# Units of one pair of edge steps, one-step message multiplies, later masks and a shifted step table in a graph-and-mixer kernel

## The chip, the cores and the metric

The kernel runs on one core of a Trainium2 chip. The metric is device time in microseconds (us); smaller is better. Everything is in fp32.

## The reference

The input `x` has 3125 rows (nodes) of 256 values. There are 53,125 edges, each with a source row, a destination row (the list is sorted by destination) and one of 400 relation types. `xn` is `x`, layer-normalised.

```python
def _mgcn_conv(x, edge_index, edge_type, rel, W_in, W_out, W_loop, b, n):
    m = x[src] * rel[edge_type]
    m = jnp.concatenate([m[:half] @ W_in, m[half:] @ W_out], 0)
    agg = jax.ops.segment_sum(m * norm[dst][:, None], dst, num_segments=n)
    return jnp.tanh(agg + x @ W_loop + b)
h = emb + res * _mgcn_conv(emb, ..., rel1, ...)
h = h + res * _mgcn_conv(h, ..., rel2, ...)
return h @ mu_w + mu_b
```

To this graph part, run on `xn`, are added `x` itself and the result of a mixer on `xn`: four layers, each of a linear attention (queries by softmax over a head's 32 columns, keys by softmax over all 3125 rows, one 32x32 context a head) and a feed-forward of 1024 hidden columns with gelu. On the sum `x`, layer-normalised once more, a last block of one shared three-layer network and four small expert networks (the two best by a softmax gate) gives what is added at the end.

## The kernel before

**Tiles.** The nodes stand in 25 tiles of 125 rows, in five groups of five. The mixer goes layer by layer (0 to 3) and in a layer group by group: `iteration(lay, gi)`, called (lay, gi) below. Ahead of each layer stands a joint, `joint(la)`, in which the context over all rows is closed and turned into weights (joint 1 stands between layers 0 and 1), and ahead of joint 0 the fronts (queries, keys and values of layer 0, one for each group). The last stage (the last block, with the second dense part of the graph) runs over slots `s = 1..26`, one tile each.

**Edges.** Each of the two graph layers (g=0 and g=1) has 416 steps of 128 edges. For a step POOL gathers 128 node rows into a ring of 16 slots by an indirect DMA (L1049: `xg<-xn_rows` for g=0, `xg<-h_rows` for g=1). For g=0 it also gathers 128 rows of relations, of both layers side by side (L1001, `rg<-relation_rows`). SP stores the second half of these to DRAM (L875, L892) and loads them back for g=1 (L917). A unit was `UNIT = 4` steps, in two pairs: one step of each pair belongs to the first 64 rows of a window of 125 nodes, the other to the last 61. For a unit DVE writes a one-hot table of its 4x64 rows (L1128, `hot`; for the first units also `hot_extra`, L1132), waits for the unit's gathers and multiplies the rows by the relations, in one instruction of 128x1024 (L1143). PE then sums the rows into windows by the one-hot table (L2735, `ps_seg`): for a pair two matmuls side by side, 64 and 61 columns wide, where its other matmuls are 125 or 128 wide. When they are done the unit's four ring slots are free for POOL (`s_seg`). Once a window is complete DVE adds it to `acc`, for each tile that it meets under a mask from the table `in_tile` (L1117).

**Order.** Every engine's order is written out. The numbers of steps beside each front, joint, group and the last stage stand in tables (`STEPS_FRONT`, `STEPS_JOINT`, `STEPS_GROUP`, `STEPS_LAST`), divided by `UNIT`; `marks`, `joint_marks`, `front_marks` and `last_units` spread a group's units over places in its work. DVE makes its units one unit ahead of PE (`units_ahead`, L738). g=0 ends in (2,3), where `AMONG` units stand among the 25 tiles of its dense part (`dense_behind`); g=1 begins in (2,4) (`dense_before`) and ends in the last stage.

**Masks.** `in_tile` needs 36 small subtractions, one for each window (L2100, 125x2), and two operations on the whole table (L2103, L2105). They stand in DVE's prologue, ahead of three `k_max` and two `norm` of the fronts (L1205, L1346). The first add that reads the table is some units later.

**Last stage.** In each slot DVE makes `gated_rows` (L2151), a share of units, and so on. For the next group of tiles its last normalisation is made in three steps: `last_stats` (L1902), at slot s when tile s+3 opens a group, and one slot later `last_root` (L1908 and the small ops of `inv_sqrt`, L548 to L567) with `last_rows` (L1918, which writes `acc`). PE transposes `acc` as the group's first work (L607).

Of the kernel before, what the change touches and what calls it, by code (L numbers as in the profile page):

```python
# [9 lines left out]
ALU = mybir.AluOpType  # L10
# [15 lines left out]
RING = 16  # L26
SLOTS = 3
CUT = 112
UNIT = 4
HOT_UNITS = 2  # L30
ROUND = 2
WIN = 6
BLOCK = 4
HEADSTART = 16
STORE_AT = (2, 5)
STRIPS = ((0, 64), (64, T))
# [3 lines left out]


STEPS_FRONT = (0, 8, 8, 8, 8)
STEPS_JOINT = (16, 16, 16, 32)
STEPS_GROUP = ((16, 24, 24, 24, 24), (16, 24, 24, 24, 24), (16, 24, 24, 48, 48), (24, 52, 52, 52, 52))
STEPS_LAST = 104
AMONG, AMONG_AT, AMONG_EVERY = 6, 3, 3
DENSE_LAYER, DENSE_GROUP = 2, 4
LAG = 18

# [1 line left out]
def build(nc, io, out):  # L51
# [133 lines left out]
    with ExitStack() as ctx:  # L185
# [540 lines left out]

        def among(t):

            return min(max((t - AMONG_AT) // AMONG_EVERY + 1, 0), AMONG)

        def dense_loads(h):

# [327 lines left out]
        def _(dve):  # L1060
# [36 lines left out]
            class Edges:  # L1097
# [23 lines left out]
                def unit(self):  # L1121
# [17 lines left out]
                    else:  # L1139
                        dve.wait_ge(s_edge[k % RU], (k // RU + 1 + 2 * (UNITS // RU)) * (16 * UNIT))  # L1140
                        dve.wait_ge(s_r2ld[k % RU], (k // RU + 1) * 16)
                        r = rg2[:, s:s + UNIT, :]
                    dve.tensor_tensor(m, m, r, ALU.mult).then_inc(s_msg, 1)  # L1143
                    while self.adds < adds_before(k):
                        self.add()
                    for _ in range(2):
# [292 lines left out]
            def front_tiles(f, before, after, m, upto, one):  # L1439

                if before:
                    before.k_max(GT - 1)
                f.norm(2)
                upto(m[0])
                f.norm(3)
                f.norm(4)
                if before:
                    before.q_max()
                    before.k_top()
                    before.q_shift()  # L1450
                upto(m[1])
                if before:
                    before.k_shift()
                f.k_max(1)
                upto(m[2])
                if before:
                    before.q_sum()
                    before.q_scale()
                f.k_max(2)
                upto(m[3])  # L1460
                if not after:
                    f.q_max(0)
                    f.q_shift(0)
                f.k_max(3)
                if after:
                    after.norm(0)
                    after.norm(1)
                upto(m[4])
                if before:
                    before.add_context()  # L1470
                if not after:
                    f.q_sum(0)
                    f.k_max(GT - 1)
                    f.q_scale(0)
# [620 lines left out]
            dve.wait_ge(s_ppe, 7)  # L2095
            p(dve.tensor_copy(starts, ps_in[0:T, 0:WINS]))
            p.wait()
            for w in range(WINS):
                a, found = in_tile_at[w], blocks_of(w)
                p(dve.tensor_scalar(in_tile[:, a:a + len(found)], row_of[:, found.start:found.stop], starts[:, w:w + 1], None,  # L2100
                                    ALU.subtract))
            p.wait()
            p(dve.tensor_scalar(below, in_tile[:, :], 0.0, None, ALU.is_ge))  # L2103
            p.wait()
            p(dve.scalar_tensor_tensor(in_tile[:, :], in_tile[:, :], strip_width, below, ALU.is_lt, ALU.mult))  # L2105
            p.wait()
            dve.sem_inc(s_tab, 1)
            fronts[0].k_max(2)
            fronts[0].k_max(3)
            fronts[1].norm(0)  # L2110
            fronts[1].norm(1)
            dve.wait_ge(s_zero, 2)

            at, edges = 0, Edges(0)
            for ga in range(1, NG):
# [55 lines left out]
            for s in range(1, NT + 2):  # L2171
# [21 lines left out]
                if gi and j == 0:  # L2193
                    softmax(gi)
                    top_two(gi)
                    gates(gi)
                if last_part(s + 3)[1] == 0:
                    rooted = last_stats(last_part(s + 3)[0])
                if last_part(s + 2)[1] == 0:
                    last_root(rooted)  # L2200
                    last_rows(last_part(s + 2)[0])


        @block.scalar
# [1318 lines left out]
```

## Time and profile before

| what | value |
|---|---|
| runs of the kernel | 1978.4 us median of 3 (1976.6 to 1980.3) |
| the profiled execution, its own time | 1990.7 us |
| its span in the trace | 1988.9 us |
| busy: PE, DVE, POOL, ACT | 1771.3, 1183.3, 1335.6, 627.8 us |
| mean granted TensorE clock | 0.961 of full |

The page gives for each engine how long it was busy, then the chain of work that ended last, then the costliest groups of instructions with what ended the idle time before them. A stretch view gives the same for a piece of the span, a timeline each instruction with its start, its duration and, in brackets, the idle time of its engine before it and what ended that. An instruction of PE stands in the timeline from its issue to its modelled end, so that consecutive rows overlap; for PE the distance from start to start is read.

### The profile page before, as it was taken

To read this page: it belongs to the slowest core of one execution; us is meant where nothing else is said; L and a number is where in the kernel's file an instruction comes from. 1 tells how busy PE (TensorE), PEld (TensorE's weight loads), DVE (VectorE), ACT (ScalarE), POOL (GpSimd) and SP (SyncE) were. 2 spreads that over 40 slices of the span, in tenths; PEclk is the share of its full clock that TensorE was granted. 3 is DMA by queue.
4 is the path that set the end of the run, shared out by engine and by line. 5 is a ranking of instruction groups with operands and counts; after the bars stand their busy time and mean duration, and the time that the engine had idled before them with its cause. 6 is when DMAs were issued, how large, how long until landed. Compare 5 with 4: busy or idle time off the path is not lost.

```text
span 1988.9 us, 27738 instructions
## 1 busy us (share of the span) xinstructions
PE 1771.3 (89%) x9423; PEld 1303.9 (66%) x9423; DVE 1183.3 (59%) x2959; ACT 627.8 (32%) x1552; POOL 1335.6 (67%) x1297
## 2 busy tenths in 40 slices
PE   2788899998899999989999879878989898988988
PEld 1455777776587777658777546646656665766778
DVE  6766455564755556474655554585455465577755
ACT  4442233443323344332333233232221222222333
POOL 6776777777777777777777716755677566677200
PEclk9898999999899999999999999998999998989989
DMA  9667666667766666776667755758656556555201
GB/s 256 185 200 238 200 186 204 187 197 217 235 196 194 205 195 192 243 217 196 193 197 218 233 146 169 226 182 221 185 185 202 162 176 189 160 175 183 82 14 27
DMA packets 195918, 371.40 MB, mean 187 GB/s; under 512 B 39343, under 2 KB 127445, under 8 KB 195780
## 3 DMA queue, kind: packets, MB, share of 16 engines
q0 software_dynamic: 74304, 220.71, 38.3%
q1 hardware_dynamic: 93124, 126.68, 20.0%
q10 hardware_dynamic: 28352, 22.24, 4.1%
q8 instruction: 78, 1.28, 0.3%
q14 instruction: 60, 0.49, 0.1%
HBM read 305.39 MB, written 64.95 MB: 186 GB/s over the span
## 4 chain that ended last, share of the span: by engine, by line
PE 43%; POOL 26%; issue 10%; DVE 10%; DMA 4%; SPq 2%; ACT 1%; ACTq 1%; DVEq 0%; POOLq 0%
POOL xg L1049 16%; POOL rg L1001 10%; PE ps_down L2876 8%; PE ps_hid L2864 7%; PE ps_seg L2735 5%; PE ps_x L607 2%; PE ps_hid L3358 2%; DMA xg<-h_rows,idx_tab 2%; PE ps_kv L2773 2%; DVE xg L1143 2%; PE ps_x L2828 2%; SPq L788 2%; PE ps_down L2906 1%; PE ps_kv L2906 1%; DMA h_rows<-qT_all 1%
## 5 line engine op out<-in xcount | busy, mean ns | idle before, releaser
L1049 POOL DMA_INDIRECT xg<-h_rows,idx_tab x416 | 444.7, 1069 | 208.6 <-issue 119.6
L1049 POOL DMA_INDIRECT xg<-xn_rows,idx_tab x416 | 437.7, 1052 | 133.4 <-issue 125.5
L1001 POOL DMA_INDIRECT rg<-relation_rows,idx_tab x416 | 429.5, 1033 | 136.4 <-issue 126.1
L2864 PE MATMUL ps_hid<-hT,wff 128*128 128x250 f32 (+1 forms) x1920 | 370.9, 346 | 9.1 <-ACT gT L2298 9.1
L2876 PE MATMUL ps_down<-wff,gT 128*125 128x256 f32 x1600 | 373.0, 387 | 0.0
L2864 PEld LDWEIGHTS ps_hid<-hT,wff 128*128 128x128 f32 x1920 | 313.4, 192 | 60.6 <-issue 28.4
L2876 PEld LDWEIGHTS ps_down<-wff,gT 128*125 128x125 f32 x1600 | 300.1, 192 | 48.8 <-issue 5.1
L1143 DVE TENSOR_TENSOR xg<-xg,rg 128x1024 f32<-128x1024 f32 x208 | 253.7, 1220 | 128.8 <-DMA rg<-relation_rows,idx_tab 67.3
L2298 ACT ACTIVATE gT<-ps_hid,b1p 128x250 f32<-128x250 f32 (+1 forms) x480 | 176.4, 433 | 294.2 <-PE ps_hid L2864 294.1
L2735 PE MATMUL ps_seg<-xg,hot 128*64 128x257 f32 (+1 forms) x1664 | 232.9, 404 | 34.8 <-DVE xg L1143 31.8
L2735 PEld LDWEIGHTS ps_seg<-xg,hot 128*64 128x64 f32 (+1 forms) x1664 | 102.6, 139 | 131.2 <-issue 57.3
L1128 DVE TENSOR_TENSOR hot<-iota_t,key_tab 128x256 f32<-128x256 f32 x208 | 87.0, 418 | 64.8 <-PE ps_seg L2735 63.2
L2773 PE MATMUL ps_kv<-wqkv,hTa 128*125 128x512 f32 x240 | 115.7, 604 | 1.8 <-ACT hTa L2238 1.8
L2209 ACT ACTIVATE kx<-ps_kv 125x256 f32<-125x256 f32 x72 | 27.7, 384 | 233.3 <-PE ps_kv L2773 221.8
L1117 DVE SCALAR_TENSOR_TENSOR acc<-ps_seg,in_tile,acc 125x257 f32<-125x257 f32 x194 | 93.2, 480 | 3.0
L1323 DVE TENSOR_TENSOR xres<-xres,ps_down 125x256 f32<-125x256 f32 x100 | 39.9, 416 | 90.7 <-PE ps_down L2876 90.1
L1265 DVE TENSOR_TENSOR xres<-xres,ps_x 125x256 f32<-125x256 f32 x80 | 30.7, 416 | 95.2 <-PE ps_x L2828 95.1
L2284 ACT ACTIVATE hT<-ps_x,ln2p 128x250 f32<-128x250 f32 (+1 forms) x120 | 56.1, 525 | 98.6 <-PE ps_x L607 93.8
L2828 PE MATMUL ps_x<-cwo,qT_all 128*125 128x256 f32 x320 | 82.1, 396 | 0.0
L1205 DVE TENSOR_TENSOR kmax<-kmax,kx 125x256 f32<-125x256 f32 x54 | 22.8, 422 | 83.6 <-ACT kx L2209 83.0
L2773 PEld LDWEIGHTS ps_kv<-wqkv,hTa 128*125 128x125 f32 x240 | 43.6, 189 | 41.6 <-issue 37.1
L2828 PEld LDWEIGHTS ps_x<-cwo,qT_all 128*125 128x125 f32 x320 | 57.7, 191 | 20.0 <-issue 12.8
(382 smaller groups left out, 2435.7 us busy)
## 6 DMA issues: line engine op xcount, KB each, us to landing
second_relation_rows<-rg SPq DMA_DIRECT2D x104, 512.0 KB, 4.1
rg<-second_relation_rows SPq DMA_DIRECT2D x104, 512.0 KB, 3.9
wff<-L_mix_W ACTq DMA_DIRECT2D x8, 1024.0 KB, 7.4
rg<-relation_rows,idx_tab POOLq DMA_INDIRECT x416
xg<-xn_rows,idx_tab POOLq DMA_INDIRECT x416
xg<-h_rows,idx_tab POOLq DMA_INDIRECT x416
h_rows<-qT_all SPq DMA_DIRECT2D x25, 64.0 KB
qrow<-h_rows ACTq DMA_DIRECT2D x25, 64.0 KB
```

Of the source, the lines that this page charges most:

```text
L1001: pool.indirect_dma_start(rg[:, k, :], None, rel_d, indices(step, 1)).then_inc(s_edge[k // UNIT], 16)
L1049: pool.indirect_dma_start(xg[:, k, 0:D], None, rows, indices(step, 0)).then_inc(s_edge[k // UNIT], 16)
L1117: dve.scalar_tensor_tensor(a, ps_seg[bank_of(w)][0:T, 0:AW], in_tile[:, m:m + 1], a, ALU.mult, ALU.add).then_inc(s_acc, 1)
L1128: dve.tensor_tensor(hot[:, hs:hs + UNIT, :], iota_t[:, :].unsqueeze(1).broadcast_to([EP, UNIT, WIDTH[0]]), key_tab[:, at:at + UNIT].unsque ...
L1143: dve.tensor_tensor(m, m, r, ALU.mult).then_inc(s_msg, 1)
L2284: ins = act.activation(hT[:, j:z, c, :], turned[:, :, c * T:(c + 1) * T], ACT.Identity, bias=ln2p[:, 1, c:c + 1], scale=ln2p[:, 0, c:c + 1])
L2298: ins = act.activation(out, hidden, ACT.Gelu, bias=b1p[:, ff:ff + 1])
L2735: ins = pe.matmul(ps_seg[bank_of(w)][a:z, 0:AW], hot[:, u % HOT_UNITS * UNIT + part, 0:z - a], xg[:, u % RU * UNIT + part, :], start=now = ...
L2773: ins = pe.matmul(ps_kv[0:T, :], hTa[:, j % 2, c, :], wqkv[:, c, 0:2 * D], start=c == 0, stop=c == KC - 1)
L2828: ins = pe.matmul(ps_b[j % 2][0:T, :], q[:, c * T:(c + 1) * T], cwo[:, c, :], start=c == 0, stop=c == KC - 1)
L2864: ins = pe.matmul(hidden, w1[:, c, ff * P:(ff + 1) * P], hT[:, a:z, c, :], start=c == 0, stop=c == KC - 1)
L2876: ins = pe.matmul(ps_down[j % 2][0:T, :], gT[:, j % 2, f, :], w2[:, f, :], start=f == 0, stop=f == FC - 1)
```

## The change

- `UNIT` 4 to 2: a unit is one pair of steps. The ring has 8 units in place of 4 (`RU`), `HOT_UNITS` 2 to 4 and `BLOCK` 4 to 2 keep the buffers at their size, and SP stores and loads 208 blocks of 256 KB in place of 104 of 512 KB. DVE's lead of one unit is now 2 steps.
- The message multiply is one instruction of 128x256 for each step, in place of 128x1024 for four.
- Layer 2's steps beside its last group, and layer 3's: joint 3 32 to 20 steps, (2,4) 48 to 52, (3,0) 24 to 36, (3,1) 52 to 40, (3,2) to (3,4) 52 to 56 each, the last stage 104 to 100. `AMONG` 6 to 12 keeps its 24 steps, at twice the units a tile.
- The masks move from the prologue into front 1: 12 after its `norm(4)`, 12 after `k_max(1)`, the rest and the two whole-table operations after `k_max(2)`.
- In the last stage `last_stats`, `last_root` and `last_rows` stand one slot earlier.

```diff
--- before.py
+++ after.py
@@ -26,11 +26,11 @@
 RING = 16
 SLOTS = 3
 CUT = 112
-UNIT = 4
-HOT_UNITS = 2
+UNIT = 2
+HOT_UNITS = 4
 ROUND = 2
 WIN = 6
-BLOCK = 4
+BLOCK = 2
 HEADSTART = 16
 STORE_AT = (2, 5)
 STRIPS = ((0, 64), (64, T))
@@ -40,10 +40,10 @@
 
 
 STEPS_FRONT = (0, 8, 8, 8, 8)
-STEPS_JOINT = (16, 16, 16, 32)
-STEPS_GROUP = ((16, 24, 24, 24, 24), (16, 24, 24, 24, 24), (16, 24, 24, 48, 48), (24, 52, 52, 52, 52))
-STEPS_LAST = 104
-AMONG, AMONG_AT, AMONG_EVERY = 6, 3, 3
+STEPS_JOINT = (16, 16, 16, 20)
+STEPS_GROUP = ((16, 24, 24, 24, 24), (16, 24, 24, 24, 24), (16, 24, 24, 48, 52), (36, 40, 56, 56, 56))
+STEPS_LAST = 100
+AMONG, AMONG_AT, AMONG_EVERY = 12, 3, 3
 DENSE_LAYER, DENSE_GROUP = 2, 4
 LAG = 18
 
@@ -726,7 +726,7 @@
 
         def among(t):
 
-            return min(max((t - AMONG_AT) // AMONG_EVERY + 1, 0), AMONG)
+            return min(max((t - AMONG_AT) * 2 // AMONG_EVERY + 1, 0), AMONG)
 
         def dense_loads(h):
 
@@ -1140,7 +1140,9 @@
                         dve.wait_ge(s_edge[k % RU], (k // RU + 1 + 2 * (UNITS // RU)) * (16 * UNIT))
                         dve.wait_ge(s_r2ld[k % RU], (k // RU + 1) * 16)
                         r = rg2[:, s:s + UNIT, :]
-                    dve.tensor_tensor(m, m, r, ALU.mult).then_inc(s_msg, 1)
+                    for i in range(UNIT):
+                        ins = dve.tensor_tensor(m[:, i, :], m[:, i, :], r[:, i, :], ALU.mult)
+                    ins.then_inc(s_msg, 1)
                     while self.adds < adds_before(k):
                         self.add()
                     for _ in range(2):
@@ -1444,6 +1446,8 @@
                 upto(m[0])
                 f.norm(3)
                 f.norm(4)
+                if f.ga == 1:
+                    make_masks(12)
                 if before:
                     before.q_max()
                     before.k_top()
@@ -1452,11 +1456,15 @@
                 if before:
                     before.k_shift()
                 f.k_max(1)
+                if f.ga == 1:
+                    make_masks(12)
                 upto(m[2])
                 if before:
                     before.q_sum()
                     before.q_scale()
                 f.k_max(2)
+                if f.ga == 1:
+                    make_masks(WINS)
                 upto(m[3])
                 if not after:
                     f.q_max(0)
@@ -2095,21 +2103,29 @@
             dve.wait_ge(s_ppe, 7)
             p(dve.tensor_copy(starts, ps_in[0:T, 0:WINS]))
             p.wait()
-            for w in range(WINS):
-                a, found = in_tile_at[w], blocks_of(w)
-                p(dve.tensor_scalar(in_tile[:, a:a + len(found)], row_of[:, found.start:found.stop], starts[:, w:w + 1], None,
-                                    ALU.subtract))
-            p.wait()
-            p(dve.tensor_scalar(below, in_tile[:, :], 0.0, None, ALU.is_ge))
-            p.wait()
-            p(dve.scalar_tensor_tensor(in_tile[:, :], in_tile[:, :], strip_width, below, ALU.is_lt, ALU.mult))
-            p.wait()
             dve.sem_inc(s_tab, 1)
             fronts[0].k_max(2)
             fronts[0].k_max(3)
             fronts[1].norm(0)
             fronts[1].norm(1)
             dve.wait_ge(s_zero, 2)
+
+            masks = [w for w in range(WINS)]
+
+            def make_masks(n):
+
+                for _ in range(min(n, len(masks))):
+                    w = masks.pop(0)
+                    a, found = in_tile_at[w], blocks_of(w)
+                    ins = dve.tensor_scalar(below[:, a:a + len(found)], row_of[:, found.start:found.stop], starts[:, w:w + 1], None,
+                                            ALU.subtract)
+                    if not masks:
+                        p(ins)
+                        p.wait()
+                        p(dve.tensor_scalar(in_tile[:, :], below, 0.0, None, ALU.is_ge))
+                        p.wait()
+                        p(dve.scalar_tensor_tensor(in_tile[:, :], below, strip_width, in_tile[:, :], ALU.is_lt, ALU.mult))
+                        p.wait()
 
             at, edges = 0, Edges(0)
             for ga in range(1, NG):
@@ -2194,11 +2210,11 @@
                     softmax(gi)
                     top_two(gi)
                     gates(gi)
+                if last_part(s + 4)[1] == 0:
+                    rooted = last_stats(last_part(s + 4)[0])
                 if last_part(s + 3)[1] == 0:
-                    rooted = last_stats(last_part(s + 3)[0])
-                if last_part(s + 2)[1] == 0:
                     last_root(rooted)
-                    last_rows(last_part(s + 2)[0])
+                    last_rows(last_part(s + 3)[0])
 
 
         @block.scalar
```

PE in group (1,1) of layer 1, before; L2864 and L2876 are the two halves of the feed-forward:

```order
L2864 MATMUL ps_hid<-hT,wff 128x250 x8
L2735 MATMUL ps_seg<-xg,hot 64x257
L2735 MATMUL ps_seg<-xg,hot 61x257
L2735 MATMUL ps_seg<-xg,hot 64x257
L2735 MATMUL ps_seg<-xg,hot 61x257
L2864 MATMUL ps_hid<-hT,wff 128x250 x8
L2735 MATMUL ps_seg<-xg,hot 64x257
L2735 MATMUL ps_seg<-xg,hot 61x257
L2735 MATMUL ps_seg<-xg,hot 64x257
L2735 MATMUL ps_seg<-xg,hot 61x257
L2876 MATMUL ps_down<-wff,gT 125x256 x8
```

The same place now (the lines are 16 further down):

```order
L2880 MATMUL ps_hid<-hT,wff 128x250 x4
L2751 MATMUL ps_seg<-xg,hot 64x257
L2751 MATMUL ps_seg<-xg,hot 61x257
L2880 MATMUL ps_hid<-hT,wff 128x250 x4
L2751 MATMUL ps_seg<-xg,hot 64x257
L2751 MATMUL ps_seg<-xg,hot 61x257
L2880 MATMUL ps_hid<-hT,wff 128x250 x8
L2751 MATMUL ps_seg<-xg,hot 64x257
L2751 MATMUL ps_seg<-xg,hot 61x257
L2892 MATMUL ps_down<-wff,gT 125x256 x8
L607 MATMUL ps_x<-ident,kx 128x125 x2
```

The two units of two pairs each are four units of one pair, each alone between other matmuls: where PE went over to the narrow shape and back twice, it now does so four times.

DVE in layer 1, before; L1198, L1205, L1265 and L1323 are work of the mixer:

```order
L1198 TENSOR_SCALAR kx<-xres,mv,rstd 125x256
L1128 TENSOR_TENSOR hot<-iota_t,key_tab 128x256
L1143 TENSOR_TENSOR xg<-xg,rg 128x4x256
L1198 TENSOR_SCALAR kx<-xres,mv,rstd 125x256
L1205 TENSOR_TENSOR kmax<-kx 125x256
L1265 TENSOR_TENSOR xres<-xres,ps_x 125x256 x2
L1323 TENSOR_TENSOR xres<-xres,ps_down 125x256
L1198 TENSOR_SCALAR kx<-xres,mv,rstd 125x256
L1205 TENSOR_TENSOR kmax<-kmax,kx 125x256
L1128 TENSOR_TENSOR hot<-iota_t,key_tab 128x256
L1143 TENSOR_TENSOR xg<-xg,rg 128x4x256
L1117 SCALAR_TENSOR_TENSOR acc<-ps_seg,in_tile,acc 125x257 x3
```

The same place now:

```order
L1200 TENSOR_SCALAR kx<-xres,mv,rstd 125x256
L1128 TENSOR_TENSOR hot<-iota_t,key_tab 128x128
L1144 TENSOR_TENSOR xg<-xg,rg 128x256 x2
L1128 TENSOR_TENSOR hot<-iota_t,key_tab 128x128
L1144 TENSOR_TENSOR xg<-xg,rg 128x256 x2
L1200 TENSOR_SCALAR kx<-xres,mv,rstd 125x256
L1207 TENSOR_TENSOR kmax<-kx 125x256
L1267 TENSOR_TENSOR xres<-xres,ps_x 125x256 x2
L1325 TENSOR_TENSOR xres<-xres,ps_down 125x256
L1200 TENSOR_SCALAR kx<-xres,mv,rstd 125x256
L1207 TENSOR_TENSOR kmax<-kmax,kx 125x256
L1128 TENSOR_TENSOR hot<-iota_t,key_tab 128x128
```

The table of a unit is 128x128 in place of 128x256, and its multiply two instructions of 128x256 in place of one of 128x1024; other work of DVE stands between the two halves of what was a unit, or the halves follow each other.

DVE at the second group of the last stage, before:

```order
L1128 TENSOR_TENSOR hot<-iota_t,key_tab 128x256
L1143 TENSOR_TENSOR xg<-xg,rg 128x4x256
L1871 SCALAR_TENSOR_TENSOR qrow<-kx,singles,qrow 125x256
L1879 TENSOR_TENSOR xres<-xres,ps_kv 125x256
L1847 TENSOR_SCALAR kmax<-acc,norm 125x256
L2167 TENSOR_TENSOR xres<-xres,ps_down 125x256
L2161 SCALAR_TENSOR_TENSOR xres<-kx,xres 125x256 x4
L1908 BN_AGGR mv<-stat 125x2 x5
L548 TENSOR_SCALAR var<-mv 125x5
```

The same step now (L1908 is now L1916, L2151 is now L2167, L1863 and L1871 are 8 further down):

```order
L1128 TENSOR_TENSOR hot<-iota_t,key_tab 128x128
L1144 TENSOR_TENSOR xg<-xg,rg 128x256 x2
L1117 SCALAR_TENSOR_TENSOR acc<-ps_seg,in_tile,acc 125x257
L1128 TENSOR_TENSOR hot<-iota_t,key_tab 128x128
L1144 TENSOR_TENSOR xg<-xg,rg 128x256 x2
L1871 TENSOR_TENSOR kx<-ps_kv,gb 125x256
L2183 TENSOR_TENSOR xres<-xres,ps_down 125x256
L2177 SCALAR_TENSOR_TENSOR xres<-kx,xres 125x256 x4
L1916 BN_AGGR mv<-stat 125x2 x5
L548 TENSOR_SCALAR var<-mv 125x5
```

The aggregation stood behind the `qrow` rows of a dense tile in the slot of the third `gated_rows`; it now stands in the slot of the second, behind the `kx<-ps_kv` row that precedes them.

## Rows read from the trace of the kernel before

**Rows 1.** The page: busy time by engine, and the chain by engine.

```profile
PE 1771.3 (89%) x9423; PEld 1303.9 (66%) x9423; DVE 1183.3 (59%) x2959; ACT 627.8 (32%) x1552; POOL 1335.6 (67%) x1297
...
PE 43%; POOL 26%; issue 10%; DVE 10%; DMA 4%; SPq 2%; ACT 1%; ACTq 1%; DVEq 0%; POOLq 0%
```

**Rows 2.** Stretches: start:end, length, busy us (instructions) by engine, PEclk, DMA share, GB/s.

```profile
320.00:385.00 65.00, 63.46 (x321) 47.64 (x320) 38.83 (x96) 25.05 (x60) 50.42 (x48) 1.00 0.66 195
655.80:719.00 63.20, 62.87 (x319) 47.47 (x319) 38.87 (x95) 24.97 (x59) 48.89 (x47) 1.00 0.67 197
...
1405.00:1500.00 95.00, 79.20 (x417) 57.54 (x416) 47.46 (x94) 16.37 (x41) 72.58 (x68) 0.93 0.65 201
1720.00:1989.00 269.00, 237.24 (x1659) 197.71 (x1657) 180.15 (x484) 79.50 (x262) 98.05 (x88) 0.93 0.33 100
1758.40:1765.10 6.70, 3.89 (x15) 2.05 (x16) 5.98 (x19) 1.14 (x3) 5.15 (x5) 0.50 0.38 103
```

**Rows 3.** Waits of PE in 1405 to 1500 and in 1720 to 1989: total, times, longest.

```profile
PE ps_seg L2735 <- DVE xg L1143: 11.2, 6, 2.5
...
PE ps_down L607 <- DVE acc L1918: 12.2, 4, 4.8
```

**Rows 4.** Groups by line: busy us, mean ns, idle before by releaser.

```profile
L1049 POOL DMA_INDIRECT xg<-h_rows,idx_tab x416 | 444.7, 1069 | 208.6 <-issue 119.6 <-PE ps_seg L2735 84.4 <-DMA h_rows<-qT_all 4.6
L1049 POOL DMA_INDIRECT xg<-xn_rows,idx_tab x416 | 437.7, 1052 | 133.4 <-issue 125.5 <-PE ps_seg L2735 6.4 <-DMA xn_rows<-xres 1.5
L1001 POOL DMA_INDIRECT rg<-relation_rows,idx_tab x416 | 429.5, 1033 | 136.4 <-issue 126.1 <-DVE idx_tab L1083 10.0 <-DMA xn_rows<-xres 0.3
...
L1143 DVE TENSOR_TENSOR xg<-xg,rg 128x1024 f32<-128x1024 f32 x208 | 253.7, 1220 | 128.8 <-DMA rg<-relation_rows,idx_tab 67.3 <-DMA xg<-h_rows,idx_tab 57.9 <-DMA xg<-xn_rows,idx_tab 3.0
```

**Rows 5.** Timeline 690.9 to 696: start, us, engine, line, op, [idle before <-releaser].

```profile
691.26 0.94 POOL L1049 DMA_INDIRECT xg<-xn_rows,idx_tab  x1 [0.30 <-issue]
...
692.45 1.22 DVE L1143 TENSOR_TENSOR xg<-xg,rg 128x1024 f32<-128x1024 f32 x1
692.51 1.98 POOL L1001 DMA_INDIRECT rg<-relation_rows,idx_tab  x1 [0.30 <-issue]
```

**Rows 6.** Timeline 713 to 716, DVE and POOL.

```profile
713.72 0.42 DVE L1128 TENSOR_TENSOR hot<-iota_t,key_tab 128x256 f32<-128x256 f32 x1
713.84 1.12 POOL L1001 DMA_INDIRECT rg<-relation_rows,idx_tab  x1 [0.30 <-issue]
714.06 1.22 DVE L1143 TENSOR_TENSOR xg<-xg,rg 128x1024 f32<-128x1024 f32 x1
```

**Rows 7.** Timeline 604 to 612 and 620 to 646, PE.

```profile
604.53 3.62 PE L2876 MATMUL ps_down<-wff,gT 128*125 128x256 f32 x16
...
608.08 1.09 PE L2735 MATMUL ps_seg<-xg,hot 128*64 128x257 f32 x8
...
609.09 1.99 PE L2828 MATMUL ps_x<-cwo,qT_all 128*125 128x256 f32 x8
...
641.49 3.62 PE L2876 MATMUL ps_down<-wff,gT 128*125 128x256 f32 x16
...
644.94 0.38 PE L607 MATMUL ps_x<-ident,xh 125*128 125x125 f32 x2
```

**Rows 8.** Timeline 45 to 60, the prologue on DVE and PE.

```profile
47.81 4.81 DVE L2100 TENSOR_SCALAR in_tile<-qT_all 125x2 f32<-125x2 f32 x36
...
54.73 0.40 PE L607 MATMUL ps_x<-ident,wff 125*128 125x125 f32 x2 [3.84 <-DVE wff L1346]
```

**Rows 9.** Timeline 480 to 492, the second joint.

```profile
484.13 1.23 DVE L1143 TENSOR_TENSOR xg<-xg,rg 128x1024 f32<-128x1024 f32 x1 [9.83 <-DMA rg<-relation_rows,idx_tab]
...
486.84 0.79 PE L2785 MATMUL ps_kv<-ident,ktop 128*125 128x128 f32 x2 [5.57 <-DVE ktop L1212]
```

**Rows 10.** Timeline 1757 to 1762.5, the last stage.

```profile
1760.64 1.84 DVE L1918 TENSOR_SCALAR acc<-xres,mv,rstd 125x256 f32<-125x256 f32 x5
...
1761.11 0.68 PE L607 MATMUL ps_down<-ident,acc 125*128 125x125 f32 x2 [4.83 <-DVE acc L1918]
```

## The prediction

> **What bounds the kernel now.** I read the page first: PE is busy for 1771.3 us of the span of 1988.9, POOL for 1335.6, DVE for 1183.3, and the chain that ended last runs 43% over PE and 26% over POOL's gathers [rows 1]. PE is idle for 1988.9 - 1771.3 = 217.6 us; this is all that better timing can give back. Then I read the stretches [rows 2]. An iteration of layer 0 takes 65.0 us with PE busy for 63.46, one of layer 1 63.2 with 62.87: layer 1 is bound by PE, layer 0 nearly so. In layer 3's first part PE is busy for 79.20 of 95 us at a granted clock of 0.93, in the last stage for 237.24 of 269. So the reader should see two kinds of stretch: full ones, in which extra PE work is paid and nothing is gained by faster gathers, and loose ones, in which a wait can go.
>
> **Why gathers are slow.** The three groups of gathers mean 1069, 1052 and 1033 ns [rows 4], where an undisturbed one takes 0.94 with 0.30 of gap [rows 5]. Together they are (129 + 112 + 93) ns x 416 = 139 us over 0.94 each. The timeline shows one reason: the gather at 692.51, begun 0.06 us after a message multiply of 1.22, takes 1.98, and so ends 0.82 after the multiply's end, as if it had waited for that end [rows 5]. The gather at 713.84, begun under `hot`, takes only 1.12, though the multiply follows `hot` 0.34 us later: it got in between two instructions that stand back to back [rows 6].
>
> **The change, part by part.** Sums are against the profiled execution, 1990.7 us (1988.9 of span); it stands 12.3 above the median of 1978.4, and I carry differences over.
>
> *One-step multiplies on POOL.* A gather that ends 0.82 after the multiply loses nothing if it begins in the last 0.94 - 0.82 = 0.12 us of it. One that begins in the 1.10 before loses half of that on the mean; with one gather in 1.25 us this is 1.10 x 1.10 / 2 / 1.25 = 0.48 us a multiply, 101 us for 208, an estimate. Four pieces of 0.42 (as `hot`, a 256-wide one [rows 6]) cost 4 x 0.30 x 0.30 / 2 / 1.25 = 0.14, 30 us. Saved: up to 71 us of POOL; as the rows hold only 139 for all causes I take 60, half in each graph layer. The lower bound is 0, if gathers don't get in between. In full stretches this is worth nothing; in loose ones it is counted below.
>
> *One-step multiplies and smaller tables on DVE.* From start to start `hot` occupies 0.34 [rows 6], the multiply 1.22 - 0.08 = 1.14, with the overlap of 0.08 that `hot` has. Four pieces take 4 x 0.34 = 1.36, +0.22; two tables of 128x128 in place of one of 128x256 cost between 0 and another 0.34, and I take 0.06, since a narrower one should be shorter. So 208 x 0.28 = +58 us busy, between 46 and 117, on an engine busy for 60%. It hides beside PE; where DVE feeds PE directly, joint 3 and the last stage with 120 steps (30 of the old units), it is 30 x 0.28 = 8 at most, and as DVE waits there as well I allow +3. The Trainium skill, page "VectorE: DVE Perf Modes", section "The TRN2 errata — SBUF-src ops pay a fixed extra latency per instruction", speaks against this part: many small tiles each pay a fixed price, so that by its formula (151 + N columns at 0.96 GHz, an estimate) four pieces would take 1.70 us, +98 us busy in all. All on the path in those 30 units, that would be +14 in place of +3, and with the factor of two thirds below the forecast 1962. The row's 0.34 from start to start shows part of that price hidden behind the instruction before.
>
> *Units of one pair on PE.* Sixteen full-width matmuls followed by others of full width take 644.94 - 641.49 = 3.45; followed by a unit 608.08 - 604.53 = 3.55; so going over costs 0.10. The unit takes 609.09 - 608.08 = 1.01, where four pairs at the 3.45 / 16 = 0.216 of a full matmul would be 0.86: 0.15 more [rows 7]. Coming back I take as going over, 0.10: 0.35 us a run of units. Counted in PE's order, runs that stand alone rise from 194 to 303: +109, or +38 us of PE, 83 of them (29 us) in g=0. The bounds are 0.10 (11 us) and 0.45 (49 us). The Trainium skill, page "TensorEngine Tiling (Array Packing)", section "Key Properties", says that a change of tiling mode drains the array; the rows agree, with these 0.35 us.
>
> *Masks.* PE's wait of 3.84 in the prologue is for `wff` of L1346, which stands behind the 36 masks (4.81) [rows 8]. -4, all of that wait; the 4.81 go into front 1 beside POOL's gathers and cost up to 5 there if PE waits for that front's `k_max`.
>
> *g=0.* Prologue -4. Joints 0 and 1, 2 and group (0,1) are loose: in joint 1 DVE stands for 9.83 behind a multiply for its gathers and PE for 5.57 for the `ktop` behind it [rows 9]. POOL gains some 30 us over g=0, 10 of them by then: I take -6 there, and -7 for the other places of this kind (waits for relation rows are 67.3 us in all, the 9.83 among them [rows 4]). In layer 0 the 1.54 us that PE idles in an iteration pay for five runs more (1.75): 0. Layer 1 is full: 5 x 1.7 = +8. The rest of the runs stand beside other waits: +3. Sum -6.
>
> *g=1.* POOL waits for free slots for 84.4 us in g=1 [rows 4]; moving 12 steps from (3,1) to (3,0), and 12 out of joint 3, puts gathers where the ring stands empty, and units of two steps free slots twice as often. In 1405 to 1500, (3,1), PE idles for 15.8 us, 11.2 of them for the multiply that waits for gathers [rows 2, 3]: 12 steps fewer at 1.25 are 15 us of POOL: -15. (2,4) and joint 3: -6, of the same 84.4. The other groups -2. Last stage: PE waits 12.2 us in 4 times for L1918 [rows 3], once for 4.83 us right behind it [rows 10], and after it the clock stands at 0.50 for 6.7 us with 3.89 busy [rows 2]. One slot of 269 / 25 = 10.8 us earlier covers this; -12, and half of the busy time of two or three such spells, 2 to 6, as -5: -17. Runs +5, DVE +3. Sum -32.
>
> Together -38. Each wait that goes shows what was late behind it (PE idles for 217.6, and other terms take only a sixth of this), and DVE's lead of two steps in place of four costs, below, nothing, and above, ten more waits like the 11.2 / 6 = 1.9 us of PE for the multiply [rows 3], 20. As no row excludes either, I keep two thirds of the gain, -24: **1954.4 us**.
>
> **The rivals.**
> - *PE pays for the runs and gets nothing back in g=0.* The +38 us fall where PE is the bound; joints wait for other things than POOL. For it: layer 1 is full, and 83 of 109 runs are in g=0 [rows 2]. Then g=0 is -4 + 29 = +25, g=1 with half its gains -13: +12, 1990. It decides once the recovered waits are under the 38 us of the runs. This is the slower side.
> - *Gathers don't get in between the pieces.* Four multiplies back to back hold them off like one of 1.22. The page "SBUF — State Buffer" of the Trainium skill, section "🔬 SBUF: two separate sides", has a lock held for a whole instruction, which speaks for a gap at its end, as does the gather at 713.84 [rows 6]. Without the 13 of the joints and a third of the 21 in layer 3, times two thirds: -24 + 13 = -11, 1967.
> - *DVE's lead is too short.* PE comes to a unit whose gathers and multiply are not quite done, twice as many units as before; a dozen more waits of 1.9 us [rows 3] eat the 24: 0, 1978. It decides from there on.
> - *All waits go at once*, with the half clock behind them: -38 and 12 more where the clock of 0.93 in the two loose stretches rises [rows 2] (0.07 x 316 us of busy PE is 22, of which 10 are counted): -50, 1928.
>
> **How the numbers follow.** My forecast (1942 to 1968) has 0.46; all waits at once 0.12; gathers held off 0.14; the short lead 0.10, which splits over no change (0.07) and slightly slower (0.03); PE's runs 0.18, of them 0.01 within no change. A measurement can tell 0.2%, 4 us. So faster 0.46 + 0.12 + 0.14 = 0.72, same 0.08, slower 0.20. The range reaches from the case of all waits to that of the runs, 1928 to 1990, a little out at the low end for the POOL saving's bound: 1925 to 1990. The likeliest case's own range is 1942 to 1968.
>
> **What would show it.** Right: gathers near 0.97 us on the mean, few of 1.5 or more; PE's wait for L1918 gone and the clock 1.0 there; 1405 to 1500 with PE over 90% busy; the iteration of layer 1 longer by 1 to 2 us; PE's busy time up by about 30; DVE's by 46 to 60. Wrong: PE waiting for L1143 (now 208 pairs) longer in all than before, or gathers as long as now, or a layer 0 that doesn't shrink anywhere while layer 1 grows by 8.

## The result, and the profile after

The changed kernel takes 1992.0 us (median of 9 runs, 1987.7 to 2001.0), the kernel before 1980.3 in the same comparison (9 runs, 1975.7 to 1990.0). The ratio is 1.0062, 95% interval 1.0037 to 1.0087: **slower by 0.6%, 12 us**, where 1954 was forecast.

The two traces don't show this at a glance: the profiled execution of before (1990.7) was one of its slowest, that of the change (1988.6) one of its fastest. Differences of stretches are good to some ten microseconds in all, and medians decide on the whole. First the page's busy times of the change, then its groups by line, the answer to [rows 1, 4]:

```profile
PE 1796.5 (90%) x9423; PEld 1284.9 (65%) x9423; DVE 1236.0 (62%) x3803; ACT 629.7 (32%) x1552; POOL 1293.8 (65%) x1297
```

```profile
L1001 POOL DMA_INDIRECT rg<-relation_rows,idx_tab x416 | 427.6, 1028 | 135.9 <-issue 126.1 <-DVE idx_tab L1083 9.4 <-DMA xn_rows<-xres 0.3
L1049 POOL DMA_INDIRECT xg<-xn_rows,idx_tab x416 | 424.0, 1019 | 131.0 <-issue 120.0 <-PE ps_seg L2751 5.5 <-DMA xn_rows<-xres 4.6
L1049 POOL DMA_INDIRECT xg<-h_rows,idx_tab x416 | 418.6, 1006 | 251.4 <-PE ps_seg L2751 135.0 <-issue 109.8 <-DMA h_rows<-qT_all 6.3
...
L1144 DVE TENSOR_TENSOR xg<-xg,rg 128x256 f32<-128x256 f32 x832 | 313.8, 417 | 26.5 <-DMA xg<-h_rows,idx_tab 13.5 <-DMA rg<-relation_rows,idx_tab 6.5 <-DMA xg<-xn_rows,idx_tab 5.4
...
L2751 PE MATMUL ps_seg<-xg,hot 128*64 128x257 f32 (+1 forms) x1664 | 263.6, 412 | 66.7 <-DVE xg L1144 63.4 <-DVE acc L1117 1.7 <-DVE acc L1114 1.3
```

PE is busy for 1796.5 us in place of 1771.3, and idle for 190 in place of 218. The gathers are shorter by 41.7 us together (418.6 + 424.0 + 427.6 against 1311.9). But PE's waits for a message multiply (L1144, before L1143) are now 63.4 us, where they were 31.8: the prediction had named longer waits there as a sign of being wrong.

To find where the time went I followed the same matmuls of PE through both traces. The change is ahead by 13 us at the end of group (0,1), by 25 behind joint 1, by 18 behind layer 1 and by 44 where the last stage's matmuls begin, at 1665.1 in place of 1709.2. Then it loses all of it. These are stretches of the change: an iteration of layer 0, one of layer 1, the part of layer 3 that stood at 1405 to 1500, and the last stage (start:end, length, busy us (instructions) of PE, PEld, DVE, ACT and POOL, then PEclk, DMA share, GB/s):

```profile
306.00:370.90 64.90, 64.57 (x321) 47.01 (x320) 40.47 (x121) 25.02 (x58) 50.28 (x49) 1.00 0.67 194
630.00:694.80 64.80, 64.47 (x320) 47.01 (x321) 40.37 (x120) 25.27 (x59) 49.82 (x49) 1.00 0.67 200
1383.60:1461.20 77.60, 75.71 (x419) 54.51 (x418) 49.19 (x154) 17.57 (x45) 55.76 (x54) 1.00 0.69 204
1665.10:1986.80 321.70, 261.90 (x1712) 211.47 (x1710) 189.59 (x587) 81.28 (x267) 89.58 (x92) 0.91 0.30 86
```

And of the kernel before, cut at the same matmuls, an iteration of layer 1, the part of layer 3 and the last stage:

```profile
651.10:714.30 63.20, 62.87 (x319) 47.47 (x319) 38.84 (x96) 24.97 (x59) 48.89 (x48) 1.00 0.66 197
1405.00:1502.10 97.10, 81.30 (x427) 59.31 (x426) 47.88 (x95) 16.37 (x41) 74.24 (x70) 0.93 0.65 199
1709.20:1988.90 279.70, 248.04 (x1716) 206.52 (x1714) 182.73 (x490) 82.38 (x267) 104.19 (x95) 0.93 0.33 100
```

Layer 1's iteration went from 63.2 to 64.8, layer 0's stayed (65.0 before [rows 2]), layer 3's piece went from 97.1 us with a clock of 0.93 to 77.6 at full clock. **The last stage went from 279.7 to 321.7: +42 us**, with PE idle for 60 us in place of 32. The waits in it, of the change (total, times, longest):

```profile
POOL xg L1049 <- PE ps_seg L2751: 80.9, 26, 6.8
DVE xh L2167 <- PE ps_x L3455: 69.2, 21, 5.8
...
PE ps_seg L2751 <- DVE xg L1144: 47.3, 25, 5.9
```

Before, the wait of the last row was, in the last stage:

```profile
PE ps_seg L2735 <- DVE xg L1143: 5.1, 5, 2.0
```

A timeline of two places in it (start, us, engine, line, op, [idle before <-releaser]):

```profile
1699.03 0.65 PE L2751 MATMUL ps_seg<-xg,hot 128*64 128x257 f32 x4
...
1700.59 1.72 DVE L1910 BATCH_NORM_STATS2 stat<-xres 125x6 f32<-125x256 f32 x5
...
1702.42 0.76 DVE L1144 TENSOR_TENSOR xg<-xg,rg 128x256 f32<-128x256 f32 x2
...
1703.29 0.76 DVE L1144 TENSOR_TENSOR xg<-xg,rg 128x256 f32<-128x256 f32 x2
1703.32 0.65 PE L2751 MATMUL ps_seg<-xg,hot 128*64 128x257 f32 x4 [3.64 <-DVE xg L1144]
...
1716.18 0.65 PE L2751 MATMUL ps_seg<-xg,hot 128*64 128x257 f32 x4
...
1717.55 0.44 DVE L1916 BATCH_NORM_AGGREGATE mv<-stat 125x2 f32<-125x6 f32 x5
...
1720.14 1.70 DVE L1926 TENSOR_SCALAR acc<-xres,mv,rstd 125x256 f32<-125x256 f32 x5
...
1721.97 0.75 DVE L1144 TENSOR_TENSOR xg<-xg,rg 128x256 f32<-128x256 f32 x2
...
1722.77 1.12 PE L2751 MATMUL ps_seg<-xg,hot 128*64 128x257 f32 x4 [5.94 <-DVE xg L1144]
```

A slot of this stage has two places for units (`last_units`), one in each half. A half slot has some two units of two steps where it had one of four, and the lead of one unit covers only the first. PE's first matmuls of a pair run at once (1699.03, 1716.18). For the second PE stands until DVE has come to the next pair of units: behind five statistics (1700.59) it waits for 3.64, and behind the chain of the earlier normalisation (1717.55 to 1720.14 and 1.70 more) for 5.94, after which a unit takes nearly twice as long (1.12 for 0.65). The granted clock of the stretch behind it is 0.58, so that most of it ran at the lower level of 1.2 GHz:

```profile
1722.70:1729.40 6.70, 6.63 (x34) 5.80 (x36) 0.90 (x5) 1.69 (x6) 1.89 (x2) 0.58 0.41 117
```

DVE for its part stands for a matmul of PE further on in the slot (L2167, 69.2 us), and POOL for free ring slots (80.9).

### The profile page after: what moved, and what is told of

The parts are those of the page before. It is cut to its first block and busy times, and to the rows that moved or that the text cites. A ratio compares the mean times of both kernels' runs of the same rounds, so it can differ in the third digit from the quotient of the medians.

```text
span 1986.8 us, 29094 instructions
## 1 busy us (share of the span) xinstructions
PE 1796.5 (90%) x9423; PEld 1284.9 (65%) x9423; DVE 1236.0 (62%) x3803; ACT 629.7 (32%) x1552; POOL 1293.8 (65%) x1297
## 5 line engine op out<-in xcount | busy, mean ns | idle before, releaser
L1049 POOL DMA_INDIRECT xg<-h_rows,idx_tab x416 | 418.6, 1006 | 251.4 <-PE ps_seg L2751 135.0
L1001 POOL DMA_INDIRECT rg<-relation_rows,idx_tab x416 | 427.6, 1028 | 135.9 <-issue 126.1
L1049 POOL DMA_INDIRECT xg<-xn_rows,idx_tab x416 | 424.0, 1019 | 131.0 <-issue 120.0
L2880 PE MATMUL ps_hid<-hT,wff 128*128 128x250 f32 (+1 forms) x1920 | 381.3, 349 | 6.6 <-ACT gT L2314 6.3
L2892 PE MATMUL ps_down<-wff,gT 128*125 128x256 f32 x1600 | 363.2, 380 | 0.0
L1144 DVE TENSOR_TENSOR xg<-xg,rg 128x256 f32<-128x256 f32 x832 | 313.8, 417 | 26.5 <-DMA xg<-h_rows,idx_tab 13.5
L2751 PE MATMUL ps_seg<-xg,hot 128*64 128x257 f32 (+1 forms) x1664 | 263.6, 412 | 66.7 <-DVE xg L1144 63.4
L2892 PEld LDWEIGHTS ps_down<-wff,gT 128*125 128x125 f32 x1600 | 293.2, 188 | 45.4 <-issue 5.1
L2751 PEld LDWEIGHTS ps_seg<-xg,hot 128*64 128x64 f32 (+1 forms) x1664 | 90.2, 137 | 183.3 <-issue 82.3
L1128 DVE TENSOR_TENSOR hot<-iota_t,key_tab 128x128 f32<-128x128 f32 x416 | 117.7, 283 | 25.0 <-PE ps_seg L2751 23.4
L1117 DVE SCALAR_TENSOR_TENSOR acc<-ps_seg,in_tile,acc 125x257 f32<-125x257 f32 x194 | 93.2, 481 | 38.6 <-PE ps_seg L2751 30.9
```

The source lines that it names most:

```text
L1001: pool.indirect_dma_start(rg[:, k, :], None, rel_d, indices(step, 1)).then_inc(s_edge[k // UNIT], 16)
L1049: pool.indirect_dma_start(xg[:, k, 0:D], None, rows, indices(step, 0)).then_inc(s_edge[k // UNIT], 16)
L1117: dve.scalar_tensor_tensor(a, ps_seg[bank_of(w)][0:T, 0:AW], in_tile[:, m:m + 1], a, ALU.mult, ALU.add).then_inc(s_acc, 1)
L1128: dve.tensor_tensor(hot[:, hs:hs + UNIT, :], iota_t[:, :].unsqueeze(1).broadcast_to([EP, UNIT, WIDTH[0]]), key_tab[:, at:at + UNIT].unsque ...
L1144: ins = dve.tensor_tensor(m[:, i, :], m[:, i, :], r[:, i, :], ALU.mult)
L2751: ins = pe.matmul(ps_seg[bank_of(w)][a:z, 0:AW], hot[:, u % HOT_UNITS * UNIT + part, 0:z - a], xg[:, u % RU * UNIT + part, :], start=now = ...
```

## The experiments

All ratios are to the kernel before, 1975.8 to 1977.5 us in these comparisons. Runs 1, 4, 6 and 8 were measured together, so were 3, 7, 9 and the first of 11, and 2, 5, 10 and the second of 11; across these sets the ratios compare better than the medians.

**1. Two units of lead in the last stage.**

```diff
-            upto, _ = edges.stage(at_last, 1)
+            upto, _ = edges.stage(at_last, 2)
```

> DVE makes its units two units (four steps) ahead of PE in the last stage, as many steps as in the kernel before; all else as in the change. If the short lead is what costs the 42 us that the change loses in the last stage, PE's waits there for the multiply (47.3 us in 25 times) fall under 15 and the time falls by 30 to 45, to 1947 to 1962, below the kernel before. If the normalisation one slot earlier is the cause, or the runs of units on PE, the waits stay and the time stays within 6 us of 1992.

Measured: 1946.6 us, ratio 0.982 (0.979 to 0.986). PE's instructions and their order are those of the change; only DVE makes its units earlier. Its last stage, and PE's wait in it:

```profile
1670.30:1945.60 275.30, 248.58 (x1712) 203.29 (x1710) 188.65 (x587) 81.83 (x267) 91.93 (x92) 0.94 0.34 100
```

```profile
PE ps_seg L2751 <- DVE xg L1144: 14.3, 8, 4.1
```

275.3 us in place of 321.7, the wait 14.3 in place of 47.3. This one number turns the change from 0.6% slower into 1.8% faster than the kernel before: the lead is what made it slower.

**2. The adds alone.** The change with its lead of one unit, and DVE's window adds (L1117) allowed only four units behind its own unit, which is eight steps as in the kernel before:

```diff
-                        if self.adds < ADDS and last_unit(add_list[self.adds][0]) <= k - 2:
+                        if self.adds < ADDS and last_unit(add_list[self.adds][0]) <= k - 4:
```

> The change itself, with its lead of one unit everywhere, and only the window adds allowed four units behind. If the lead of two steps is what costs the last stage its 42 us, this gains no more than the adds gave with the longer lead: 0 to 16, to 1976 to 1992, and PE's waits for the multiply in the last stage stay over 35 us. If the adds that DVE stands at are what delays the multiplies there, most of the 45 comes back: 1945 to 1955.

Measured: 1975.9 us, ratio 0.999 (0.996 to 1.001). The last stage stays long, by the same waits:

```profile
1650.10:1967.90 317.80, 259.36 (x1712) 209.61 (x1710) 189.48 (x587) 81.30 (x267) 91.86 (x95) 0.92 0.31 88
```

```profile
PE ps_seg L2751 <- DVE xg L1144: 46.0, 25, 5.9
```

So the adds are not what delays the multiplies there. The 16 us that they give come for the most part ahead of the last stage, which begins 15 us earlier than in the change and is 3.9 shorter.

**3. Adds four units behind, with the lead of two in the last stage** (the edits of runs 1 and 2 together).

> The run with two units of lead in the last stage, with DVE's window adds allowed only four units behind its own unit in place of two, which is eight steps as in the kernel before. DVE stood for 31 us (20 times) for PE's sums at these adds, where the kernel before stood for 3. If those stands cost time, 3 to 12 less than 1947; if DVE has slack there, within 4 us.

Measured: 1930.6 us, ratio 0.976 (0.974 to 0.978), 16 less than run 1 (13 by the ratios): more than expected. DVE's stands for PE's sums at L1117, 31.1 us in run 1, are gone from the trace, so they did cost time. That the thresholds are counted in units, which the change halved, is the second thing that it lost by.

**4. Two units of lead everywhere** (the edit of run 1, and the joints and groups too).

```diff
-            return 0 if (lay, gi) == (0, 0) or dense_before(lay, gi) else 1
+            return 0 if (lay, gi) == (0, 0) or dense_before(lay, gi) else 2
...
-                joint_rest = joint(lay, *edges.stage(at_joint[lay], min(lay, 1)))
+                joint_rest = joint(lay, *edges.stage(at_joint[lay], 2 * min(lay, 1)))
```

> Two units of lead in the joints and the mixer's groups too. By the theory of the short lead this adds to the run with the lead in the last stage alone only what PE waits for the multiply elsewhere (63.4 - 47.3 = 16 us at most): 0 to 10 less. By the rival that DVE must not be sent to wait for gathers earlier (other work of DVE then stands behind that wait), it is up to 10 slower than that run.

Measured: 1989.3 us, ratio 1.006 (1.004 to 1.008): 43 slower than run 1, far beyond the 10 that I allowed. DVE's wait at the adds, in the whole span:

```profile
DVE acc L1117 <- PE ps_seg L2751: 143.0, 44, 8.1
```

In run 1 it was 31.1 in 20 times. The threshold lets DVE, at its unit k, add a window that ends with unit k - 2. With two units of lead PE has only come to that unit, and DVE stands until its sum is done.

**5. Both: two units of lead everywhere, and adds four units behind** (the edits of runs 4 and 2).

> Two units of lead in joints, groups and the last stage, with the window adds four units behind. The run with the long lead everywhere (1989) had DVE standing 143 us (44 times) at its adds for PE's sums, against 31 with the long lead in the last stage alone. If that standing is the whole reason why it lost 43 us, it goes with the later adds, and this comes to within 8 us of the run with the later adds and the lead in the last stage alone (1931). If going to wait for gathers earlier is the reason, it stays at 1970 to 1990.

Measured: 1949.9 us, ratio 0.985 (0.982 to 0.988). The stand at the adds has gone from the trace, and the time is 39 under run 4's. It is still 19 over run 3's, so the adds were not the whole reason. The traces differ in layer 3, where DVE now waits for 41.8 us (31 times) for PE to free a one-hot table (L1128), against 14.1 (12 times) in run 3; that this is the cause was not tried.

**6. Units of two pairs, all else of the change kept.**

```diff
-UNIT = 2
-HOT_UNITS = 4
+UNIT = 4
+HOT_UNITS = 2
...
-BLOCK = 2
+BLOCK = 4
...
-AMONG, AMONG_AT, AMONG_EVERY = 12, 3, 3
+AMONG, AMONG_AT, AMONG_EVERY = 6, 3, 3
```

> The change with units of two pairs (and the buffers, blocks and the dense part's units of before): one-step multiplies, later masks, the shifted steps and the earlier normalisation stay. If the units of one pair are what made the change slower, by their lead in the last stage (42 us) and by 109 runs more on PE (up to 38), this is faster than the change by 40 to 60: 1932 to 1952. If the finer units bring more elsewhere (slots freed earlier, half the gathers to wait for) than their runs cost, it is 1950 to 1965. If the earlier normalisation or the step table is at fault, it stays at 1985 to 1995.

Measured: 1944.4 us, ratio 0.983 (0.980 to 0.986); the last stage is 265.7 us long:

```profile
1677.30:1943.00 265.70, 241.14 (x1708) 200.47 (x1706) 185.96 (x560) 81.81 (x267) 93.28 (x91) 0.96 0.34 102
```

So the other parts together are worth 33 us, and the units of one pair cost some 46 as they stand in the change; with the lead mended (run 1, 1946.6) they cost nothing that these runs can tell. That the 33 are near the sum that I had for g=1 confirms none of its terms: taken one by one, runs 8 to 11 give the multiplies 8, the normalisation 5 to 11, the table 2 to 4 and the masks nothing that can be told. These were tried on other kernels than this one, and where the rest of the 33 comes from is not shown.

**7. PE takes units two at a time** (run 3, and PE's own order rounds each place down to whole pairs of units; DVE, POOL and SP keep units of one pair).

```diff
-                        while self.done < base + k:
+                        while self.done < (base + k) // 2 * 2:
```

> As the run with the adds four units behind, and PE takes its units two at a time: runs of units on PE fall from 303 to 195, DVE, POOL and SP keep units of one pair. By the price of 0.35 us a run PE's busy time falls by 25 to 38 us and layer 1 by 7 to 8 us; the whole by 8 to 20 against the run with the adds alone. If slots freed twice as often are worth more to POOL than the runs cost PE, it is 0 to 10 slower.

Measured: **1915.3 us, ratio 0.969 (0.967 to 0.970)**, the fastest of all: 62 us under the kernel before. Runs of units on PE (units that follow each other without other matmuls between them) fall from 303 to 195. Busy times, first of run 3, then of this one:

```profile
PE 1784.3 (92%) x9423; PEld 1279.6 (66%) x9423; DVE 1237.0 (64%) x3803; ACT 632.8 (33%) x1552; POOL 1311.7 (68%) x1297
```

```profile
PE 1752.9 (92%) x9423; PEld 1292.4 (68%) x9423; DVE 1239.3 (65%) x3803; ACT 627.3 (33%) x1552; POOL 1304.7 (68%) x1297
```

PE is busy for 31.4 us less, 0.29 us for each of 108 runs, at equal clocks (0.972 in both). Half of it, 15 us, comes out in the time. Taking a unit later also lengthens DVE's lead, so the whole of the 15 can't be put down to the runs.

**8. The kernel before with the one-step multiplies alone.**

```diff
-                    dve.tensor_tensor(m, m, r, ALU.mult).then_inc(s_msg, 1)
+                    for i in range(UNIT):
+                        ins = dve.tensor_tensor(m[:, i, :], m[:, i, :], r[:, i, :], ALU.mult)
+                    ins.then_inc(s_msg, 1)
```

> The kernel before with the one-step multiplies alone. If gathers get in between the pieces, the mean gather falls from 1051 ns to about 1010, the joints' waits for gathers shrink, and the time falls by 10 to 20, to 1960 to 1970. If they don't, or if the added 46 us of DVE eat it, it stays within 4 us of 1980.

Measured: 1970.3 us, ratio 0.996 (0.993 to 0.998): some 8 us, less than expected. The gathers:

```profile
L1049 POOL DMA_INDIRECT xg<-xn_rows,idx_tab x416 | 426.3, 1025 | 136.2 <-issue 124.3 <-PE ps_seg L2737 11.9
L1049 POOL DMA_INDIRECT xg<-h_rows,idx_tab x416 | 423.4, 1018 | 224.4 <-issue 120.3 <-PE ps_seg L2737 99.5 <-DMA h_rows<-qT_all 4.3
L1001 POOL DMA_INDIRECT rg<-relation_rows,idx_tab x416 | 416.1, 1000 | 136.2 <-issue 126.1 <-DVE idx_tab L1083 9.8 <-DMA xn_rows<-xres 0.3
```

They are 46 us shorter (1311.9 to 1265.8), and 47 of them take 1.5 us or more, where 109 did. In this trace 138 gathers begin in a piece that another piece follows at once; 110 of them end within 0.9 us of the end of their own piece, most of them 0.82 after it, as the gather of [rows 5] ended 0.82 after the whole multiply. So gathers do get in between the pieces, and the rival that they are held off falls. The Trainium skill's page "SBUF — State Buffer", section "🔬 SBUF: two separate sides", has a lock that is held for the whole instruction; the trace agrees, with these 0.82 us behind each piece. Little of the 46 us is on the path.

**9. The last normalisation back at its old slots** (run 1 otherwise).

```diff
-                if last_part(s + 4)[1] == 0:
-                    rooted = last_stats(last_part(s + 4)[0])
-                if last_part(s + 3)[1] == 0:
+                if last_part(s + 3)[1] == 0:
+                    rooted = last_stats(last_part(s + 3)[0])
+                if last_part(s + 2)[1] == 0:
                     last_root(rooted)
-                    last_rows(last_part(s + 3)[0])
+                    last_rows(last_part(s + 2)[0])
```

> The run with two units of lead in the last stage, with the three steps of the last normalisation back at their old slots. If the earlier normalisation brings what the prediction allowed, this is 12 to 17 slower than that run (1947): 1958 to 1964, with PE's waits of some 4.8 us for the normalised rows (four times) back. If the chain is hidden anyway, or only moves the wait to the units behind it, it is within 4 us of 1947.

Measured: 1952.0 us, ratio 0.988 (0.986 to 0.990). PE's waits for the normalised rows are back, 21 us of them, where run 1 has 3.5:

```profile
PE ps_down L607 <- DVE acc L1926: 12.9, 3, 5.7
...
PE ps_x L607 <- DVE acc L1926: 8.1, 2, 4.6
```

But the time is only 5 longer than in run 1 by the medians, 11 by the ratios, and the two intervals meet at 0.986: between the two expectations, and neither is excluded. Part of this wait hid others: PE's waits for the multiply are 22.5 us in all here and 30.0 in run 1.

**10. The step tables of the kernel before** (run 1 otherwise).

```diff
-STEPS_JOINT = (16, 16, 16, 20)
-STEPS_GROUP = (..., (16, 24, 24, 48, 52), (36, 40, 56, 56, 56))
-STEPS_LAST = 100
+STEPS_JOINT = (16, 16, 16, 32)
+STEPS_GROUP = (..., (16, 24, 24, 48, 48), (24, 52, 52, 52, 52))
+STEPS_LAST = 104
```

> The run with two units of lead in the last stage, with the step tables of the kernel before (joint 3 32, layer 3 24 and 52, the last stage 104). The prediction puts 15 to 23 us on the table: 1962 to 1970. If units of two steps free the slots early enough by themselves, it is within 5 us of 1947.

Measured: 1948.6 us, ratio 0.985 (0.981 to 0.988), the same as run 1. The stretch from 1400 to 1500, first of run 1, then of this one:

```profile
1400.00:1500.00 100.00, 95.00 (x527) 69.38 (x526) 60.93 (x196) 20.47 (x50) 74.47 (x73) 0.98 0.70 203
```

```profile
1400.00:1500.00 100.00, 91.88 (x486) 65.19 (x484) 58.44 (x180) 18.13 (x46) 76.57 (x77) 0.95 0.76 221
```

Layer 3's first part is looser with the old table, and the same matmul there comes 14 us later (1512.32 for 1498.60). Where the last stage's matmuls begin 6 us of this are left, and at its end 2. POOL's waits for free slots over g=1, from which the prediction took the gain, are 94.1 us in run 1 and 94.2 here: the table moved them, and nearly nothing else.

**11. The masks back in the prologue**, once on run 1 and once on run 7: the three calls of `make_masks` in front 1 go, and the prologue has its old lines.

```diff
+            for w in range(WINS):
+                a, found = in_tile_at[w], blocks_of(w)
+                p(dve.tensor_scalar(in_tile[:, a:a + len(found)], row_of[:, found.start:found.stop], starts[:, w:w + 1], None,
+                                    ALU.subtract))
...
             dve.sem_inc(s_tab, 1)
```

> The run with two units of lead in the last stage, with the masks back in the prologue. If later masks give back in front 1 what they save in the prologue (the two profiles show -4.1 us at the prologue's end and 0 again at 77 us), this is within 4 us of 1947. By the prediction's term it is 4 slower, 1951.

> The run with PE taking its units two at a time (1915) with the masks back in the prologue. With the masks back alone 1940 was measured against 1947, of which the intervals allow 0 to 10: so 1905 to 1915. If the masks in front 1 are hidden here, where DVE waits for relation rows anyway, 1913 to 1919.

Measured: 1940.1 us, ratio 0.981 (0.979 to 0.983) against run 1's 0.982; and 1918.1, 0.970 (0.968 to 0.973) against run 7's 0.969. Both pairs of intervals overlap, and the medians point opposite ways: the masks' place makes no difference that can be told, though 4 us are not excluded. In the trace of the change PE no longer waits 3.84 us in the prologue [rows 8], but 4.08 for the first unit's multiply, and that multiply itself waits 5.43 for its gathered rows:

```profile
57.76 0.76 DVE L1144 TENSOR_TENSOR xg<-xg,rg 128x256 f32<-128x256 f32 x2 [5.43 <-DMA xg<-xn_rows,idx_tab]
...
58.67 0.65 PE L2751 MATMUL ps_seg<-xg,hot 128*64 128x257 f32 x4 [4.08 <-DVE xg L1144]
```

## Why the prediction was wrong, point by point

- **The step that failed is the lead's:** "DVE's lead of two steps in place of four costs, below, nothing, and above, ten more waits like the 11.2 / 6 = 1.9 us". The size of a wait was right (47.3 / 25 = 1.9), their number was not: 25 in the last stage alone, and behind the longest of them spells of a lower clock. The order itself tells it: `last_units` gives two units a half slot, one unit of lead covers one of them, and some 24 half slots with units make some 24 waits. I priced a lead by the waits that the old trace showed, where I had to count the places at which PE's units outnumber it. Run 1 shows the price: 45 us.
- **A term that the sum left out:** the threshold of the window adds, which is counted in units as well. DVE's stands at L1117 were 3.0 us before and 38.6 in the change, and eight steps in place of four are worth 13 to 16 us (run 2 against the change, run 3 against run 1). With lead and threshold mended the change stands at 1930.6, 46 under the kernel before, where the whole sum before the discount was 38.
- **Last stage -17:** it was +42. With units of two pairs it is 265.7 us (run 6), 14 under before's 279.7. That this is near the 17 is in part luck: the earlier normalisation itself brought 5 to 11 us, with intervals from 0 to 22 (run 9), and what gave the rest is not shown. In the change the normalisation stands in front of a unit that PE waits for.
- **Units on PE:** 0.35 us a run was estimated from two places, 0.29 was measured over 108 runs (run 7). Layer 1's iteration was to grow by 1.7 and grew by 1.6; layer 0's stayed, as forecast. Of the 109 further runs the traces have 89 in g=0, where the prediction counted 83. The Trainium skill's page "TensorEngine Tiling (Array Packing)", section "Key Properties", says that a change of tiling mode drains the array. The trace agrees in so far as a run costs 0.29 us, going over and coming back together; that a drain is what takes them no run here shows.
- **POOL:** 60 us were taken, 41.7 measured; the mean gather is 1018 ns, not 970, and 55 take 1.5 us or more, where 109 did. What the multiplies alone are worth is 8 us (run 8); the rest of POOL's gain did not come out in the time.
- **Joints:** joint 1 came as argued. DVE's wait for relation rows was 9.83 and PE's for `ktop` 5.57 [rows 9]; now the first is 0.47 and the second is gone (with the one-step multiplies alone, run 8, DVE's waits for relation rows are 19.0 us in all, where they were 67.3):

```profile
461.88 0.76 DVE L1144 TENSOR_TENSOR xg<-xg,rg 128x256 f32<-128x256 f32 x2 [0.47 <-DMA rg<-relation_rows,idx_tab]
...
467.87 0.48 PE L2801 MATMUL ps_kv<-ident,ktop 128*125 128x128 f32 x2
```

- **Masks -4:** none that can be told (run 11), and a wait of the same size at the first unit. I had named a cost in front 1, up to 5, and taken none of it.
- **Layer 3 -15 by the table:** the traces show the gain there, but of 14 us only 2 are left at the end (run 10). POOL's waits for slots over g=1 are as long with the old table, so the table did not shorten them.
- **DVE +58:** +52.7 (1236.0 for 1183.3). By the formula of the Trainium skill's page "VectorE: DVE Perf Modes", section "The TRN2 errata — SBUF-src ops pay a fixed extra latency per instruction", I had estimated +98. The trace agrees with the formula on the duration of one piece (417 ns, 424 by it), but not with four of them added up, since pieces back to back overlap; the rows' distance from start to start was the better price.
- **The rivals:** the time came out near the 1990 of the rival of PE's runs, but not by its mechanism: g=0 was to lose 25 us, and in the trace the change is ahead by 18 behind layer 1. The mechanism was that of the short lead, with 0.10 and an end at no change.

## What to carry to other kernels

When a unit of work is made smaller, everything counted in units shrinks with it: leads, thresholds, lags. Go through each and ask how much work it still covers; where a lead does not cover all units that the consumer takes in one place, the consumer can come to wait once for every such place, as PE did here (25 waits in 24 half slots). And the engines need not have the same unit: the fastest kernel here has units of one pair on POOL and DVE and takes them two at a time on PE (1915.3 us in run 7, where units of two pairs on all engines gave 1944.4 in run 6).

## What was not expected of the hardware

A gather that begins in a multiply ends in most cases 0.82 us after that multiply's end, and gets in at the seam of two that stand back to back (run 8); but the 46 us that POOL, busy for two thirds of the span, gained by this gave 8 in the time. PE's wait of 5.94 us at 1722.77 is followed by 6.7 us at a granted clock of 0.58 (a unit takes 1.12 for 0.65 us); behind the wait of 3.64 the unit still takes 0.65, and the 6.7 us from 1703.3 have 0.75. The idling of the last stage thus costs more than itself: 59.8 us of it came with 261.9 us of busy time at a mean clock of 0.91, where the same matmuls in run 1 took 248.6 at 0.94 with 26.7 of idling.
